# Four layered attention networks on one core: the plain attentions go in pairs of tiles, through parts of TensorE's array

## The reference

```python
logits = einsum('bhqd,bhkd->bhqk', qh, kh) / sqrt(16)      # + mask * -1e9, or -inf where masked
out = einsum('bhqk,bhkd->bhqd', softmax(logits), vh)       # then @ wo + bo, residual, layer norm
```

## Time and profile before

| | us |
|---|---|
| median of 3 runs (2271.86 to 2274.15) | 2272.07 |
| profiled execution, its own time | 2274.92 |
| its span, first to last instruction | 2273.2 |
| TensorE busy | 1921.8 |
| VectorE busy | 1307.1 |
| POOL busy | 996.9 |
| ScalarE busy | 967.8 |
| TensorE's mean granted clock, share of full | 0.899 |

### The profile page before, as it was taken

One profiled execution on the slowest core, in us unless ns is written; L12 is line 12 of the kernel. 1 busy time (PEld: TensorE's weight loads), 2 busy tenths in 40 slices (PEclk: granted clock), 3 DMA queues, 4 the chain that ended last, 5 costly groups with the idle time before them and its releaser, 6 DMA issues.

```text
span 2273.2 us, 32499 instructions
## 1 busy us (share of the span) xinstructions
PE 1921.8 (85%) x10497; PEld 1507.4 (66%) x10497; DVE 1307.1 (57%) x2218; ACT 967.8 (43%) x2274; POOL 996.9 (44%) x1235
## 2 busy tenths in 40 slices
PE   4666667677887887887999899998988999999997
PEld 3565556454664655664777677777766787787776
DVE  5877778658558558658444465454533635436361
ACT  1111221224334333334546465564644665556563
POOL 5566665535335336345333454434533423333330
PEclk8889998677877887887999999999988999999999
DMA  7100000000200000000000200000000000000000
GB/s 216 69 5 5 9 5 5 5 1 6 79 1 5 5 0 5 5 0 5 6 1 6 79 0 9 0 5 5 1 5 5 6 6 0 5 23 0 9 1 10
DMA packets 31292, 34.88 MB, mean 15 GB/s; under 512 B 3196, under 2 KB 30040, under 8 KB 30808
## 3 DMA queue, kind: packets, MB, share of 16 engines
q1 hardware_dynamic: 31192, 33.70, 4.8%
HBM read 31.60 MB, written 2.10 MB: 15 GB/s over the span
## 4 chain that ended last, share of the span: by engine, by line
PE 60%; DVE 11%; issue 4%; POOL 2%; ACT 2%; DVEq 0%; POOLq 0%; ACTq 0%
PE ps L503 31%; PE ps L670 9%; PE ps L701 8%; PE ps L680 6%; PE ps L514 3%; DVE xn L874 2%; DVE rowmax L1010 1%; DVE rowsum L1016 1%; PE ps L696 1%; PE ps L668 1%; DVE work L1012 1%; DVE work L1004 1%; DVE O L845 1%; POOL x_all L1126 1%; DVE stats L864 0%
## 5 line engine op out<-in xcount | busy, mean ns | idle before, releaser
L503 PE MATMUL ps<-hT,w_slot 128*128 128x256 f32 x1856 | 455.1, 399 | 21.1 <-ACT hT L744 21.1
L503 PEld LDWEIGHTS ps<-hT,w_slot 128*128 128x128 f32 x1856 | 359.7, 199 | 77.8 <-ACT hT L744 24.0
L1190 POOL TENSOR_TENSOR work<-KT,own_head 128x512 f32<-128x512 f32 x256 | 261.5, 1047 | 288.6 <-ACT KT L756 234.3
L680 PEld LDWEIGHTS ps<-ident,work 128*128 128x128 f32 x1536 | 206.4, 154 | 178.3 <-issue 110.6
L670 PE MATMUL ps<-work,QT 128*128 128x512 f32 x512 | 276.5, 622 | 22.8 <-POOL work L1190 20.6
L680 PE MATMUL ps<-ident,work 128*128 128x128 f32 x1536 | 265.5, 301 | 35.6 <-POOL work L1199 35.6
L1199 POOL TENSOR_SCALAR work<-work,winv 128x128 f32<-128x128 f32 x512 | 184.9, 384 | 218.9 <-DVE winv L1029 218.4
L886 DVE TENSOR_TENSOR x_all<-ps,x_all 128x512 f32 (+1 forms) x88 | 60.7, 690 | 379.6 <-PE ps L503 326.9
L829 ACT ACTIVATE work<-work,rowmax 128x128 f32<-128x128 f32 x768 | 245.0, 392 | 68.1 <-DVE rowmax L1008 66.5
L701 PEld LDWEIGHTS ps<-V,work 128*128 128x128 f32 x2048 | 251.2, 192 | 7.4 <-issue 4.4
L701 PE MATMUL ps<-V,work 128*128 128x17 f32 x2048 | 248.9, 254 | 2.4 <-ACT work L818 2.4
(11 more groups left out here) (119 smaller groups left out, 3015.6 us busy)
## 6 DMA issues: line engine op xcount, KB each, us to landing
ctx_in<-in_ctx SPq DMA_DIRECT2D x32, 256.0 KB, 2.7
w_slot<-in_L_xattn_W SPq DMA_DIRECT2D x2, 1024.0 KB, 6.4
w_slot<-in_L_xattn_ff_w SPq DMA_DIRECT2D x1, 2048.0 KB, 11.2
w_slot<-in_L_xattn_ffn_w SPq DMA_DIRECT2D x2, 1024.0 KB, 9.9
w_slot<-in_L_xattn_w SPq DMA_DIRECT2D x2, 1024.0 KB, 9.3
out<-x_all SPq DMA_DIRECT2D x8, 256.0 KB, 2.1
x_all<-in_x SPq DMA_DIRECT2D x1, 1536.0 KB, 11.7
pad<-in_mask_Bx1x1xS_fk SPq DMA_DIRECT2D x1, 1024.0 KB, 6.7
```

Source lines behind the costliest of these rows:

```text
L503: mm = pe.matmul(dst, lhsT(k), rhs(k), start=(k == 0), stop=(k == chunks - 1))
L680: mm = pe.transpose(bank(2 + u % 2)[:, tok(h)], prob[u % NP][:, tok(h)], ident[:, :])
L1190: pool.tensor_tensor(KB[u % NK].rearrange("p (h k) -> p h k", h=HU), keys, own_head[:, half * HU:(half + 1) * HU].unsqueeze(2).broadcast_t ...
```

## The change

It touches the plain attentions only; the quantised ones keep their order.

- Keys are spread once for two tiles. The mask `own_quad` is the sum of the masks of the two head groups, so block h holds head h of the upper 64 rows and head h of the lower 64 rows.
- Scores of two tiles are made together: two column parts times two halves of 64 rows, each a product of 256 columns; the upper half goes to bank 0, the lower to bank 1. The pair waits for what both tiles waited for.
- V has 32 columns a head (16 features, 16 ones) and is now the stationary operand; the turned weights move (128 columns). The four heads of a tile go to the four strips of 32 columns of the array, outputs lie turned in the bank, the sums repeated in 16 rows. The zeros and ones of the buffer are set once, and the buffer of the quantised values lies in the same memory.
- ScalarE copies the bank of a sequence to `staged` (two of the eight `prob` buffers; six are left for the tiles) and TensorE turns it back with four transposes into the same bank. `outputs(j)` reads from there.
- The order on TensorE is by pairs: at even i scores(i, i+1), values(i-4, i-3), turns(i-2, i-1). The staging copies stand at steps 6 and 10 of ScalarE, behind the exponentials of that step; turning back at steps 7 and 11, outputs at 8 and 12.

```diff
-        V = two("V", [P, G, H, DH + 1])
+        V = two("V", [P, G, H, 2 * DH])
...
+        Vzb = [v.rearrange("p g h d -> p (g h d)")[:, 0:G * D].bitcast(BF16).rearrange("p (g a x d) -> p g a x d", g=G, x=4, d=DH) for v in V]
...
+        own_quad = sb("own_quad", [P, HU])
+        own_quad_b = sb("own_quad_b", [P, HU], BF16)
...
+        staged = prob[NP - G:NP]
...
+        NPF = NP - G
+        STAGE_AT = [U - 2, U + 2]
+        BACK_AT = [U - 1, U + 3]
...
-                def scores(u):
-                    j, m = u // UJ, u % UJ // 2
+                np_ = None if quant else phase("natt", layer, g, mix, st)
+                def scores_free(u):
...
-                    if quant:
-                        half = slice(u % 2 * (P // 2), (u % 2 + 1) * (P // 2))
-                        pe.matmul(bank(u % 2), QTb[st][half, m, tok(j)], KBb[u // 2][half, :], start=True, stop=True).then_inc(s["scores_ps"], 1)
-                    else:
-                        pe.matmul(bank(u % 2), QT[st][:, m, tok(j)], KB[u % NK], start=True, stop=True).then_inc(s["scores_ps"], 1)
+                def scores(u):
+                    j, m = u // UJ, u % UJ // 2
+                    half = slice(u % 2 * (P // 2), (u % 2 + 1) * (P // 2))
+                    scores_free(u)
+                    pe.matmul(bank(u % 2), QTb[st][half, m, tok(j)], KBb[u // 2][half, :], start=True, stop=True).then_inc(s["scores_ps"], 1)
+                def scores_pair(u):
+                    j, m = u // UJ, u % UJ // 2
+                    scores_free(u)
+                    scores_free(u + 1)
+                    for part in range(2):
+                        cols = slice(part * 2 * S, (part + 1) * 2 * S)
+                        for e in range(2):
+                            half = slice(e * (P // 2), (e + 1) * (P // 2))
+                            mm = pe.matmul(bank(e)[:, cols], QT[st][half, m, tok(j)], KB[u // 2][half, cols], start=True, stop=True)
+                            if part:
+                                mm.then_inc(s["scores_ps"], 1)
...
-                            mm = pe.matmul(bank(4 + j)[:, hh * width:(hh + 1) * width], PT[u % 2][:, tok(h)], V[st][:, j, hh, :],
+                            mm = pe.matmul(bank(4 + j)[h * 32:(h + 1) * 32, u % UJ * S:(u % UJ + 1) * S], V[st][:, j, hh, :], PT[u % 2][:, tok(h)],
                                            start=True, stop=True)
                     mm.then_inc(s["o_ps"], 1)
+                def turn_back(j):
+                    pe.wait_ge(s["staged_ready"], G * np_ + j + 1)
+                    for b in range(UJ):
+                        mm = pe.transpose(bank(4 + j)[:, tok(b)], staged[j][:, tok(b)], ident[:, :])
+                    mm.then_inc(s["back_ps"], 1)
+                def pair_step(i):
+                    if i % 2 == 0 and i < U:
+                        scores_pair(i)
+                    for u in (i - 4, i - 3):
+                        if i % 2 == 0 and 0 <= u < U:
+                            values(u)
+                    for u in (i - 2, i - 1):
+                        if i % 2 == 0 and 0 <= u < U:
+                            turn(u)
+                    if i in BACK_AT:
+                        turn_back(BACK_AT.index(i))
+                if not quant:
+                    return pair_step
...
-                            src = prob[i % NP] if "mask" in arg else bank(i % 2)
+                            src = prob[i % NPF] if "mask" in arg else bank(i % 2)
...
-                                ex = act.activation(prob[i % NP][:, tok(h)], src[:, tok(h)], ACT.Exp, bias=shifts[:, at:at + 1])
+                                ex = act.activation(prob[i % NPF][:, tok(h)], src[:, tok(h)], ACT.Exp, bias=shifts[:, at:at + 1])
+                    if not quant and i in STAGE_AT:
+                        j = STAGE_AT.index(i)
+                        act.wait_ge(s["o_ps"], U * ap + UJ * (j + 1))
+                        act.activation(staged[j], bank(4 + j), ACT.Copy).then_inc(s["staged_ready"], 1)
...
+                            if j == 0 and layer == 2 and n["att"] == 0 and isinstance(g, int) and g == 0:
+                                dve.memset(V[st][:, :, :, DH:2 * DH], 1.0).then_inc(s["ones_set"], 1)
+                                dve.wait_ge(s["ones_set"], st + 1)
...
-                    dve.wait_ge(s["PT_ps"], U * ap + u + 1 - NP)
+                    dve.wait_ge(s["PT_ps"], U * ap + (u + 1 - NP if quant or 2 <= u < NPF else u - 1 if u < 2 else u + 1 - NPF))
...
+                    dve.wait_ge(s["back_ps"], G * np_ + j + 1)
+                    o = bank(4 + j).rearrange("p (h d) -> p h d", h=H)
+                    nth = G * np_ + j + 1
...
-                    if 0 <= u < U and u % UJ == UJ - 1:
+                    if quant and 0 <= u < U and u % UJ == UJ - 1:
                         outputs(u // UJ)
+                    if not quant and i - 1 in BACK_AT:
+                        outputs(BACK_AT.index(i - 1))
...
-                    pool.wait_ge(s["scores_ps"], U * ap + u + 1 - NK)
-                    keys = KT[st][:, m, tok(j)].unsqueeze(1).broadcast_to([P, HU, S])
-                    pool.tensor_tensor(KB[u % NK].rearrange("p (h k) -> p h k", h=HU), keys,
-                                       own_head[:, half * HU:(half + 1) * HU].unsqueeze(2).broadcast_to([P, HU, S]), ALU.mult)\
-                        .then_inc(s["KB_ready"], 1)
+                    pool.wait_ge(s["scores_ps"], U * ap + u - 6)
+                    keys = (KTb if quant else KT)[st][:, m, tok(j)].unsqueeze(1).broadcast_to([P, HU, S])
+                    own = (own_quad_b if quant else own_quad)[:, :].unsqueeze(2).broadcast_to([P, HU, S])
+                    pool.tensor_tensor((KBb if quant else KB)[u // 2].rearrange("p (h k) -> p h k", h=HU), keys, own, ALU.mult)\
+                        .then_inc(s["KB_ready"], 2)
...
-                        if not quant or u % 2 == 0:
+                        if u % 2 == 0:
```

More of the change, by code:

```diff
@@ L104 @@
 PER_PASS["local_phase"] = [ST * n for n in PER_PASS["local"]]
+PER_PASS["natt_phase"] = [ST * (a - q) for a, q in zip(PER_PASS["att"], PER_PASS["qatt"])]
 PER_PASS["masked_phase"] = [ST * sum("mask" in arg for _, arg in layer) for layer in STEPS]
-FROM_ONE = ("post", "yadd", "tin", "ffn",  "mix_phase", "att_phase", "local_phase")
+FROM_ONE = ("post", "yadd", "tin", "ffn",  "mix_phase", "att_phase", "natt_phase", "local_phase")
 BEFORE = {k: [(k in FROM_ONE) + NG * sum(PER_PASS[k][:n]) for n in range(NL + 1)] for k in PER_PASS}
@@ L234, in program @@
         xc = [b[:, :, :, :].rearrange("p a c t -> p (a c t)").bitcast(FP32).rearrange("p (g d) -> p g d", g=G) for b in QKb]
-        Vzb = two("Vzb", [P, G, H // 2, 4, DH], BF16)
+        Vzb = [v.rearrange("p g h d -> p (g h d)")[:, 0:G * D].bitcast(BF16).rearrange("p (g a x d) -> p g a x d", g=G, x=4, d=DH) for v in V]
         hid = sb("hid", [P, FC, T])
@@ L679, in turn @@
                     for h in range(HU):
-                        mm = pe.transpose(bank(2 + u % 2)[:, tok(h)], prob[u % NP][:, tok(h)], ident[:, :])
+                        mm = pe.transpose(bank(2 + u % 2)[:, tok(h)], prob[u % (NP if quant else NPF)][:, tok(h)], ident[:, :])
                     mm.then_inc(s["PT_ps"], 1)
@@ L993, in shift @@
                     sc = bank(u % 2).rearrange("p (h k) -> p h k", h=HU)
-                    pr = prob[u % NP].rearrange("p (h k) -> p h k", h=HU)
+                    pr = prob[u % (NP if quant else NPF)].rearrange("p (h k) -> p h k", h=HU)
                     shift_u = shifts[:, u * HU:(u + 1) * HU]
                     dve.wait_ge(s["scores_ps"], U * ap + u + 1)
-                    dve.wait_ge(s["PT_ps"], U * ap + u + 1 - NP)
+                    dve.wait_ge(s["PT_ps"], U * ap + (u + 1 - NP if quant or 2 <= u < NPF else u - 1 if u < 2 else u + 1 - NPF))
                     if masked:
@@ L1032, in outputs @@
                 def outputs(j):
-                    dve.wait_ge(s["o_ps"], U * ap + UJ * (j + 1))
                     if quant:
+                        dve.wait_ge(s["o_ps"], U * ap + UJ * (j + 1))
                         dve.tensor_scalar(OT[st][:, :, tok(j)], bank(4 + j)[:, 0:D].rearrange("p (c t) -> p c t", c=C),
@@ L1037, in outputs @@
                         return
-                    o = bank(4 + j)[:, 0:H * (DH + 1)].rearrange("p (h d) -> p h d", h=H)
-                    nth = G * use("att_phase", layer, g, ST * mix + st) + (j + 1 - G * BEFORE["att_phase"][2])
+                    dve.wait_ge(s["back_ps"], G * np_ + j + 1)
+                    o = bank(4 + j).rearrange("p (h d) -> p h d", h=H)
+                    nth = G * np_ + j + 1
                     dve.reciprocal(oinv[:, j, :].unsqueeze(2), o[:, :, DH:DH + 1]).then_inc(s["oinv_ready"], 1)
@@ L1172, in spread @@
                 def spread(u):
-                    j, m, half = u // UJ, u % UJ // 2, u % 2
+                    j, m = u // UJ, u % UJ // 2
```

(10 more changed lines are left out.)

12 lines of the change are left out of this document (2 added, 10 removed).

## The result

| | before | after |
|---|---|---|
| median, us (runs) | 2272.74 (4) | 2384.84 (4; 2378.95 to 2387.77) |
| ratio, 95% interval | | 1.0489, 1.0468 to 1.051 |
| profiled execution, its span | 2274.92, 2273.2 | 2387.77, 2386.0 |
| TensorE's mean granted clock | 0.899 | 0.884 |

The change makes the kernel 112 us slower. Predicted were 2392, with 2285 to 2510.

The account below looks back on a forecast made before the run. The prediction took TensorE, 85% busy, to bound the kernel, with waits from the new order exceeding the work saved. 2274.9 profiled, +98 by kinds of attention, +22 for half clock, less 2.8, gave 2392 us; range 2285 to 2510.

Parts of the forecast that it names:

- step 4: First turning back in a short masked attention: it waits 2.05 us for staging, with ready products behind it on TensorE.
- step 5: End of a short masked attention: last values to staging to turning back, 0.85 us of wait.
- step 2: Scores 4,5 of a short masked attention: TensorE waits 1.1 us for masks 2 and 3 on VectorE.
- step 3: Other stream's normalised x in a short masked attention: it hangs on VectorE, and TensorE waits 1.9 us.
- No mask: Attentions without mask: a pair waits for both exponentials, about 6.2 us a pair against 4.4, +6 us per attention.
- Scores of a pair: Score products on two row halves: 8 records overlapped in 5 slots, 1.08 us; before 1.90.
- Values of a pair: Value products in strips: 16 records overlapped in 9 slots, 0.99 us; before 1.64.
- all strips and halves at once: Rival: a pair's values take 0.44 us and scores 0.86, yet waits stay; 2354 us, chance 0.12.
- The clock: TensorE at half clock after waits: 2 us in each of 8 unmasked attentions, 0.25 in others; +22 us, 0 to 70.
- TensorE's sum decides: Rival: the other stream's products fill the waits, so saved TensorE work counts; 2174 us, chance 0.13.
- f32 does not overlap: Rival: f32 products on halves and strips do not run beside each other; 2514 us, chance 0.15.
- A wash: Rival: a half of the waits is absent; 2272 us within 0.2%, chance 0.03.

Follow-up runs that it names:

- e1: The changed kernel with the first turning back two steps later in TensorE's order; 2319.02 us, ratio 1.0212.
- e9: e4 with the value product of plain attentions at step 10 instead of 9 and the last turning back at 12 instead of 11; 2266.51 us, ratio 0.9967.
- e4: The changed kernel with scores, spreads and tile-by-tile order as before, values in strips, turning back at steps 8 and 11; 2262.71 us, ratio 0.9963.
- e6: e1 with attentions without mask tile by tile, each tile's scores on one half of 64 rows; 2277.47 us, ratio 1.0029.
- e7: Against e4: each tile's scores on one half of 64 rows, keys spread once for two tiles, tile order everywhere; 2313.95 us, ratio 1.0181.
- e3: The kernel before with only TensorE's order changed to pairs, no product cut and nothing staged; 2381.38 us, ratio 1.0476.
- e2: The changed kernel without staging copies and turning back, so its output is not the right one; 2287.74 us, ratio 1.0074.
- e8: e4 with the other stream's transposes of x and all that follows one step later in networks 3 and 4; 2323.34 us, ratio 1.0209.

## Why the prediction was right

It took the waits that TensorE's order makes to be more than the work saved, and this held: 224 us more idle against 111 us less busy. By kind of attention, from first score to first score (forecast without the clock in brackets): short masked +25 (30), short without mask +31 (24), long without mask +30 (24), long masked +25 (20). Point by point:

- **The wait at the first turning back** (step 4): 2.05 laid out, 2.33 in the attention shown; e1 gives its worth, 66 us.
- **The seam** (the wait for the last staging copy, step 5): 0.85 laid out, 0.72 read, 22 us in all. e9 took it away and won nothing, so it was not worth its length.
- **The pair's wait for masks** (step 2): 1.1 laid out, 1.16 read. **The wait for x** (step 3): 1.9 laid out, 1.38 read. It did hang on VectorE: in e4, with the old order, it is still there.
- **No mask:** 6.2 us a pair laid out. In the short attention below the pairs of scores start at 1789.68, 1794.25, 1799.36 and 1806.88, 5.7 apart in the mean; the third waits 2.95 for exponentials, the fourth 1.68. The third ran at half clock (2.08 instead of 1.13):

```profile
1795.31 1.09 PE L699 MATMUL ps<-ident,work 128*128 128x128 f32 x8
1799.36 2.08 PE L687 MATMUL ps<-work,QT 64*128 64x256 f32 x8 [2.95 <-ACT work L871]
1801.37 1.08 PE L720 MATMUL ps<-work,V 128*32 128x128 f32 x16
...
1806.88 1.13 PE L687 MATMUL ps<-work,QT 64*128 64x256 f32 x8 [1.68 <-ACT work L871]
```

  From before to after, these eight attentions grew by 60.8 us (forecast 48, and 16 for the clock), the 24 masked ones by 50.0 (50 and 6). e6 confirms the first from the other side.
- **Scores of a pair:** 1.08 without the change of shape forecast, 0.98 read. **Values of a pair:** 0.99 forecast, 0.48 read. Here the term was mis-sized, by 0.51 x 128 = 65 us of TensorE's work. I had the two records of one product follow each other; in the trace the records start by fours, 6 to 7 ns apart, the next four 0.11 us after the last of them: the four strips run together. The rival *all strips and halves at once* had this, and said 27.4 for a short masked attention; at full clock it is 27.15. The Trainium skill (TensorE: Matmul & The Clock Gate, Part 3: Packing small matmuls) has such starts about 4 ns apart. The trace agrees that they run at once, but its starts are 6 to 7 ns apart, and the measured figure counts.
- **The clock:** +22 forecast, more measured. Two neighbours of the same kind, one at full clock and one that fell to half for a part:

```profile
1321.70:1348.90 27.20, 20.76 (x178) 15.23 (x178) 14.99 (x28) 18.34 (x49) 10.38 (x11) 1.00 0.00 1
1348.90:1378.90 30.00, 23.86 (x176) 17.05 (x177) 15.58 (x29) 18.46 (x49) 8.78 (x9) 0.89 0.00 1
```

  30.0 against 27.2 us for 0.11 x 2 x 30 = 6.6 us at half clock, 0.42 us for each; the two long stretches of e7 give 0.40 and 0.46. By 0.42 the 98 us more at half clock cost about 41, an estimate.
- **Luck:** the layout of the rival *all strips and halves at once*, which is near what ran (0.86 and 0.44 a pair, 0.98 and 0.48 read), adds up to 67 us where the forecast has 98; so the mis-sized term is worth about 31 us too much, most of its 65 having gone into waits. The clock is about 20 too little. The two cancelled for the most part: the mechanism is shown, the closeness of 2392 to 2385 is luck in part.
- **TensorE's sum decides:** wrong. The idle time rose by twice what the busy time fell, and e3 loses 109 us with all the work of before. But the work is not without worth: e2 against e3. **f32 does not overlap:** wrong by the trace. **A wash:** wrong.

What stays open: how much of the busy time that e3 and e8 have more (36 and 39 us for the same products) is the clock. By 0.42 for each us at half clock it is about 18 in e3 and 41 in e8, an estimate; no run held the clock fixed.

## What to carry to other kernels

A product that is cut up to run side by side saves work time, and pays only as far as the engine has other things to do meanwhile: strips in the old order took 66 us from TensorE's busy time and 10 from the kernel's. Run the old products in the new order first: here the order by itself cost 109 us. The order alone is not the whole answer either, since cut products gave 94 us of it back. With two score banks, asking for both at once turns a ring of two into none. A thing that waits at the head of an in-order engine stands before all that is ready behind it, so a reader is placed by when its operand is ready: the edit of one number was worth 66 of 112 us.

## What the runs showed of the hardware that I had not expected

- f32 products in four strips of 32 columns: 16 records in 0.48 us, where one after the other they would be 1.76; and on two halves of 64 rows 8 records of 256 columns in 0.98.
- Behind a change of shape two f32 records of 512 columns start 0.53 us apart, on one half (e7) and on all 128 rows (e4) alike; behind the old value records, without a change of shape, 0.51 (1169.90 to 1170.41 before), and 0.43 behind a turn. A single tile's scores on a half need one change of shape more than on the whole array, and this made each tile 0.15 us longer (e7 against e4).
- With such half-row scores the clock stayed at half through 30.7 us without a pause, in two of 32 attentions; in e4, whose scores use all rows, no such stretch is seen, and none in e6, which has half-row scores of single tiles in its eight attentions without mask. What keeps the clock down is not shown.
